# Where the score burst and the weighted sums stand in the rows of a dense attention stage, and where the sums are copied

## The chip, the cores and the metric

One core of a Trainium2 chip runs the whole program. A time is the device time of one execution in microseconds (us); lower is better. The engines that matter are PE (TensorE, matrix products), ACT (ScalarE), DVE (VectorE) and POOL (GpSimd). Each works through its own row of instructions in order, and they wait for each other through semaphores.

## What is computed

Two layers, each of attention and a feed-forward part, on 32 batches of 128 tokens with 256 values each. The change lies in the second layer's attention, which is dense (no mask), has 16 heads of 64, and reads the context in every batch:

```python
q = (query @ Wq + bq).reshape(b, sq, N_HEAD, KEY_DIM)
k = (key @ Wk + bk).reshape(b, key.shape[1], N_HEAD, KEY_DIM)
v = (value @ Wv + bv).reshape(b, value.shape[1], N_HEAD, VALUE_DIM)
scores = jnp.einsum('bqhd,bkhd->bhqk', q, k) / TEMP
attn = jax.nn.softmax(scores, axis=-1)
out = jnp.einsum('bhqk,bkhd->bqhd', attn, v).reshape(b, sq, N_HEAD * VALUE_DIM)
out = out @ Wo + bo + residual
mu = jnp.mean(out, axis=-1, keepdims=True)
var = jnp.var(out, axis=-1, keepdims=True)
return (out - mu) * jax.lax.rsqrt(var + EPS) * ln_gamma + ln_beta
```

Its input is a layer norm of the running sum x, and its result is added to x. Then comes a layer of routed experts.

## The kernel before

The program has four stages, one after the other: a masked attention, a feed-forward part, the dense attention (`attention1`, from about 650 us to 1293 us of the profiled execution) and the experts. Only `attention1` is touched.

`attention1` is a pipeline over the batches b = 0 to 31, with some steps ahead of it that only project, and some behind it that only finish. Each engine has a function `step(b, u, i)` whose calls are that engine's row, written out by hand; u is b modulo 4. `run_steps` writes the steps below 8 and from 28 on out one by one, and runs the twenty from 8 to 27 as a loop of four steps at a time, with b in a register.

The 16 heads of a batch are taken in four groups n of four heads. Scores are made in two bursts, g = 0 (groups 0 and 1) and g = 1 (groups 2 and 3), into the two banks of `ps_score`, and each group goes through this chain:

- PE, `scores(b, u, g)` (L1393): a burst of small products of `qT` and `kT`. It waits until the exponentials of both groups that used the two banks are done.
- DVE, `maxima(b, n)` (L1552, L1555): the row maximum, and from it `shift`.
- ACT, `exponentials(b, n)` (L1703): four ACTIVATEs that wait for `shift` and write `prob`, with the row sums.
- DVE, `divide(b, n)` (L1561, L1563): reciprocal and product.
- PE, `transposes(b, n)` (L1402), then ACT, `copy_probT(b, n)` (L1718).
- PE, `weighted(b, u, g)` (L1414): the weighted sums of two groups, into the one bank `ps_out`. It waits until `split_attn` has read the burst in front of it.
- ACT, `copy_attn(t, s, half)` (L1751) rounds `ps_out` into `attnT`, and DVE, `split_attn(t, s, half)` (L1588), takes what the rounding left over.
- PE, `output(b, u)` (L1493): 24 products with Wo for batch b - 1. It waits for both halves of that batch's `split_attn`.

In step b the groups 0 and 1 of batch b are carried up to `copy_probT`, while groups 2 and 3 of batch b - 1 are transposed and summed. In the same steps PE projects batch b + 2 (`queries` and `keys`, L1423, and `values`, L1453) through the two banks of `ps_proj`, emptied by ACT (`copy_projection`, L1725) and by DVE (`copy_values`, L1569, which waits for its `values`). `turn_x` (L1480), `copy_x` (ACT, L1733) and `split_x` (DVE, L1577) turn the input of batch b + 4; `turn_z`, `copy_z` (L1756) and `logits_of` (L1468) make the routing logits of batch b - 4. `add_residual` (L1606), `output_statistics` (L1610, L1613) and `normalise_output` (L1619 on) finish the output on DVE, with small helpers and the residual on POOL (L1357 to L1371). On odd steps `round_context` (ACT) and `split_context` (DVE, L1583) prepare context.

Of the kernel before, what the change touches and what calls it, by code (L numbers as in the profile page):

```python
# [1139 lines left out]
def attention1(nc, ident, mv2, rstd2, logits, wq_raw, wq_address, w, ctx_t, x2_dram, x3_dram, z_dram, finished):  # L1140
# [10 lines left out]
    with ExitStack() as stack:  # L1151
# [134 lines left out]
        with nc.Block() as block:  # L1286
# [97 lines left out]
            def _(pe):  # L1384
                def scores(b, u, g):
                    s, tok = u // 2, slice((u % 2) * P, (u % 2 + 1) * P)
                    if g == 0 and u % 2 == 0:
                        pe.wait_ge(qk_ready, BLKS * (b + 2))
                    if inside(b, 1, NB) or g == 1:
                        pe.wait_ge(exp_done, NU * b + 2 * g)  # L1390
                    for j, r in product(range(HB), range(2)):
                        blk, rows = HB * g + j, slice(r * KD, (r + 1) * KD)
                        last = pe.matmul(ps_score[:, r, j, :], qT[rows, s, blk, tok], kT[rows, s, blk, tok],  # L1393
                                         start=True, stop=True)
                    last.then_inc(scores_done, 1)
# [31 lines left out]
                def queries(b, u, j):  # L1427
                    if inside(b, *projects):
                        if isinstance(b, int) and b == projects[0]:
                            pe.wait_ge(w_split, 1)  # L1430
                        if j == 0 and u % 2 == 0:
                            pe.wait_ge(xnT_ready, b + 4)
                        if inside(b, -1, NB - 3):
                            pe.wait_ge(v_ready, 2 * b + 3 + j)
                        project(b, u, j, wq, xnT[:, 1 - u // 2])
# [35 lines left out]
                def turn_x(b, u):  # L1471
                    if inside(b, 4, NB - 5):
                        bank_after_logits(b)
                    elif inside(b, 2, 3):
                        pe.wait_ge(proj_ready, b - 1)
                    elif inside(b, FIRST + 1, 1):
                        pe.wait_ge(xnT_ready, b + 4)
                    pe.wait_ge(xn_ready, b + 5)
                    for k in range(ND):
                        last = pe.transpose(ps_aux[:, k * P:(k + 1) * P], xn[:, u % 2, k * P:(k + 1) * P], ident[:])  # L1480
                    last.then_inc(xnT_done, 1)
# [24 lines left out]
                def step(b, u, i):  # L1506
                    here, back = inside(b, 0, NB - 1), inside(b, 1, NB)
                    if here:
                        scores(b, u, 0)
                    queries(b, u, 0)  # L1510
                    if inside(b, 4, NB + 3):
                        turn_z(b, u)
                    if back:
                        transposes(b - 1, 2)
                        transposes(b - 1, 3)
                    queries(b, u, 1)
                    if inside(b, 4, NB + 3):
                        logits_of(b - 4)
                    keys(b, u, 0, i)
                    if inside(b, FIRST, NB - 5):  # L1520
                        turn_x(b, u)
                    if back:
                        weighted(b - 1, (u - 1) % 4, 1)
                    if here:
                        scores(b, u, 1)
                    keys(b, u, 1, i)
                    if here:
                        transposes(b, 0)
                        transposes(b, 1)
                    values(b, u, 0)  # L1530
                    if back:
                        output(b, u)
                    values(b, u, 1)
                    if here:
                        weighted(b, u, 0)

                run_steps(pe, step)

# [1 line left out]
            def _(dve):  # L1540
# [102 lines left out]
                def step(b, u, i):  # L1643

                    turn = [None if i is None else (i + 1 if u >= k else i) for k in range(4)]
                    turn_of_loop[0] = i
                    if isinstance(b, int) and b == projects[0]:
                        dve.wait_ge(bias_loaded, 16 * N_BIAS)
                    if inside(b, FIRST, NB - 5):
                        normalise(b + 4, u, None if i is None else i + 2)  # L1650
                    here, back = inside(b, 0, NB - 1), inside(b, 1, NB)
                    if back:
                        split_attn(b - 1, (u + 1) % 2, 0)
                    if here:
                        maxima(b, 0)
                        maxima(b, 1)
                    if inside(b, 2, NB + 1):
                        normalise_output(b - 2, (u + 2) % 4, turn[2])
                    if inside(b, 4, NB + 3):
                        route(b - 4)  # L1660
                    if here:
                        divide(b, 0)
                        divide(b, 1)
                    if isinstance(b, int) and (b, 0) in split_at:
                        rest_of_weights(split_at[b, 0])
                    if inside(b, FIRST, NB - 5):
                        split_x(b, u)
                    if inside(b, 3, NB + 2):
                        normalise_routed(b - 3, (u + 1) % 4, turn[3])
                    if back:  # L1670
                        split_attn(b - 1, (u + 1) % 2, 1)
                    if isinstance(b, int) and (b, 1) in split_at:
                        rest_of_weights(split_at[b, 1])
                    if u % 2 == 1 and inside(b, -3, NB - 5):
                        split_context(b, u)
                    if here:
                        maxima(b, 2)
                        maxima(b, 3)
                        divide(b, 2)
                    if inside(b, *projects):  # L1680
                        copy_values(b, u, 0)
                    if here:
                        divide(b, 3)
                    if back:
                        add_residual(b - 1, (u + 1) % 2)
                    if inside(b, *projects):
                        copy_values(b, u, 1)
                    if isinstance(b, int) and (b, 3) in split_at:
                        rest_of_weights(split_at[b, 3])
                    if back:  # L1690
                        output_statistics(b - 1, (u + 1) % 2)
# [4 lines left out]
            def _(act):  # L1696
# [61 lines left out]
                def step(b, u, i):  # L1758
                    if isinstance(b, int) and b == projects[0]:
                        act.wait_ge(bias_loaded, 16 * N_BIAS)  # L1760
                    here, back = inside(b, 0, NB - 1), inside(b, 1, NB)
                    if back:
                        copy_attn(b - 1, (u + 1) % 2, 0)
                    if here:
                        exponentials(b, 0)
                    if inside(b, 4, NB + 3):
                        copy_z(b - 4)
                    copy_projection(b, u, 0, qT, bq, 0)
                    if back:
                        copy_probT(b - 1, 2)  # L1770
                        copy_probT(b - 1, 3)
                    if here:
                        exponentials(b, 1)
                    copy_projection(b, u, 1, qT, bq, 0)
                    if isinstance(b, int) and split_at.get((b, 0)):
                        round_weights(split_at[b, 0])
                    copy_projection(b, u, 0, kT, bk, 2)
                    if inside(b, FIRST, NB - 5):
                        copy_x(b, u)
                    if back:  # L1780
                        copy_attn(b - 1, (u + 1) % 2, 1)
                    if isinstance(b, int) and split_at.get((b, 1)):
                        round_weights(split_at[b, 1])
                    if u % 2 == 1 and inside(b, -3, NB - 5):
                        round_context(b, u, i)
                    if here:
                        exponentials(b, 2)
                    copy_projection(b, u, 1, kT, bk, 2)
                    if here:
                        copy_probT(b, 0)  # L1790
                        copy_probT(b, 1)
                        exponentials(b, 3)
                    if isinstance(b, int) and split_at.get((b, 3)):
                        round_weights(split_at[b, 3])
# [599 lines left out]
```

## Time and profile before

| | us |
|---|---|
| median of 3 runs | 1632.46 (1629.01 to 1633.26) |
| the profiled execution | 1626.76 |
| its span, first to last instruction | 1625.0 |
| PE busy in the span | 1341.5 (83%) |
| DVE busy | 1220.5 (75%) |
| ACT busy | 1032.5 (64%) |
| POOL busy | 488.9 (30%) |

Shares of busy time are means over four unlike stages. For one stage the table of busy times by stretch and the timeline of each engine are read: what stands behind what, how far apart two starts are, and which instruction an idle engine was waiting for. PEld in such a table is PE's loading of weights. PE's ends are modelled, so for PE the distance between starts says more than its busy time.

### The profile page before, as it was taken

Reading aid. Unit: us, or ns where it says so; the run is one execution under the profiler, and the core shown is the slowest. Engines: PE = TensorE matmul, PEld = TensorE weight load, DVE = VectorE, ACT = ScalarE, POOL = GpSimd, SP = SyncE. Lnnn points to the kernel's source line nnn. Section 1 sums busy time; section 2 is a strip of 40 time slices with the busy share of each in tenths; the row PEclk is TensorE's granted clock in tenths of the full one; section 3 lists DMA queues with packets and bytes.
Section 4 is the critical chain, followed back from the end, with each engine's and each line's share of the span. In section 5 each row is a group of like instructions: output and inputs, shape, how many; then the busy total and the mean of one; then the engine's idle time right before and its main releaser. Section 6 shows DMA issues by size and latency. Waiting matters only on the chain. (4 is left out here: it accounts for less than half of the span.)

```text
span 1625.0 us, 36516 instructions
## 1 busy us (share of the span) xinstructions
PE 1341.5 (83%) x11579; PEld 1174.6 (72%) x11579; DVE 1220.5 (75%) x2159; ACT 1032.5 (64%) x2751; POOL 488.9 (30%) x734
## 2 busy tenths in 40 slices
PE   3688888599961059699999999999999649998897
PEld 2465555488841059689999998989898549988897
DVE  5777777668778988467777777777777679877776
ACT  2588788555588445377766666666676328877675
POOL 2433433100000001302222222222222256667665
PEclk9799999799996579799999999999999769999999
DMA  6411111000051013501111111111110257111110
GB/s 199 146 37 34 35 35 34 12 0 0 0 168 69 8 45 115 192 1 44 34 34 34 34 44 32 32 32 32 32 39 24 81 213 267 49 40 43 43 47 20
DMA packets 66243, 96.78 MB, mean 60 GB/s; under 512 B 10213, under 2 KB 57326, under 8 KB 63345
## 3 DMA queue, kind: packets, MB, share of 16 engines
q1 hardware_dynamic: 60546, 83.16, 15.4%
q0 software_dynamic: 5616, 12.60, 2.4%
q8 instruction: 44, 0.72, 0.2%
q14 instruction: 37, 0.30, 0.1%
HBM read 76.57 MB, written 21.90 MB: 61 GB/s over the span
## 5 line engine op out<-in xcount | busy, mean ns | idle before, releaser
L1703 ACT ACTIVATE c_w_raw<-c_ps_score,c_shift 128x128 f32<-128x128 f32 x512 | 184.7, 399 | 132.2 <-DVE c_shift L1555 129.6
L2096 PE MATMUL d_ps_hT<-d_zT,d_w_tile 128*128 128x128 f32 x1248 | 148.2, 278 | 1.9 <-DVE d_zT L2201 1.9
L2096 PEld LDWEIGHTS d_ps_hT<-d_zT,d_w_tile 128*128 128x128 f32 x1248 | 145.2, 195 | 2.6 <-DVE d_zT L2201 2.6
L840 PE MATMUL b_ps<-b_down_high,b_inner 128*128 128x256 f32 x384 | 71.7, 290 | 88.3 <-DVE b_inner L1122 88.3
L2267 ACT ACTIVATE d_h<-d_ps_hT,d_b1T 128x128 f32<-128x128 f32 x312 | 88.8, 367 | 64.8 <-PE d_ps_hT L2096 62.6
L2109 PE MATMUL d_ps_y<-d_w_parts,d_hT 128*128 128x256 f32 x936 | 126.3, 293 | 1.8 <-DVE d_res L2228 1.8
L840 PEld LDWEIGHTS b_ps<-b_down_high,b_inner 128*128 128x128 f32 x384 | 61.3, 196 | 88.7 <-issue 88.7
L1369 POOL TENSOR_TENSOR c_var_o<-c_mv_o,c_eps 128x1 f32<-128x1 f32 x32 | 6.8, 213 | 394.0 <-DVE c_mv_o L1613 394.0
L484 DVE TENSOR_REDUCE a_row_max<-a_ps_score 128x8 f32<-128x1024 f32 x64 | 78.0, 1219 | 57.9 <-PE a_ps_score L395 57.9
L1703 ACT ACTIVATION_READ_ACCUMULATOR c_w_raw<-c_ps_score,c_shift 128x1 f32 x512 | 121.4, 237 | 0.0
L2109 PEld LDWEIGHTS d_ps_y<-d_w_parts,d_hT 128*128 128x128 f32 x936 | 119.0, 198 | 2.4 <-DVE d_res L2228 2.0
L2220 DVE TENSOR_TENSOR d_w_parts<-d_w,d_w_parts 128x1024 fp32r<-128x1024 f32 x78 | 95.7, 1228 | 28.2 <-ACT d_w_parts L2279 26.5
L1423 PE MATMUL c_ps_proj<-c_ctxT,c_wk 128*128 128x256 f32 x768 | 106.8, 289 | 4.2 <-ACT c_qT L1725 2.9
L577 ACT ACTIVATE a_probT<-a_ps_probT 128x512 f32<-128x512 f32 x128 | 71.5, 626 | 57.1 <-PE a_ps_probT L406 56.9
L1423 PE MATMUL c_ps_proj<-c_xnT,c_wq 128*128 128x256 f32 x768 | 105.9, 289 | 1.0 <-DVE c_xnT L1577 1.0
L2279 ACT ACTIVATE d_w_parts<-d_w 128x1024 fp32r x78 | 82.2, 1054 | 34.2 <-PE d_ps_y L2109 28.8
L1423 PEld LDWEIGHTS c_ps_proj<-c_ctxT,c_wk 128*128 128x128 f32 x768 | 94.5, 191 | 10.5 <-issue 3.3
L1453 PE MATMUL c_ps_proj<-c_wv,c_ctxT 128*128 128x512 f32 x384 | 100.7, 399 | 1.1 <-DVE c_wv L1595 1.1
L1423 PEld LDWEIGHTS c_ps_proj<-c_xnT,c_wq 128*128 128x128 f32 x768 | 94.6, 192 | 5.1 <-issue 1.4
L1561 DVE RECIPROCAL c_inv_sum<-c_row_sum 128x4 f32<-128x4 f32 x128 | 22.5, 176 | 99.5 <-ACT c_w_raw L1703 99.1
L866 ACT ACTIVATE b_act<-b_ps 128x512 f32 (+1 forms) x96 | 56.7, 601 | 61.9 <-PE b_ps L805 57.2
L1493 PEld LDWEIGHTS c_ps_aux<-c_wo,c_attnT 128*128 128x128 f32 x768 | 92.1, 188 | 4.4 <-issue 1.9
(263 smaller groups left out, 3747.4 us busy)
## 6 DMA issues: line engine op xcount, KB each, us to landing
d_w<-w_in SPq DMA_DIRECT2D x16, 1024.0 KB, 12.2
b_x_space<-w_in SPq DMA_DIRECT2D x16, 512.0 KB, 3.5
a_x<-x_in SPq DMA_DIRECT2D x4, 1024.0 KB, 8.0
a_keys<-ctx_blocks_in SPq DMA_DIRECT2D x128, 32.0 KB, 2.1
a_v_raw<-ctx_in SPq DMA_DIRECT2D x4, 1024.0 KB, 9.0
x_scratch<-a_x SPq DMA_DIRECT2D x32, 128.0 KB, 1.7
b_x_space<-x_scratch SPq DMA_DIRECT2D x32, 128.0 KB, 2.3
x_scratch<-b_x_space SPq DMA_DIRECT2D x32, 128.0 KB, 1.9
```

Of the source, the lines that this page charges most:

```text
L484: dve.tensor_reduce(row_max[:, half, :], ps_score[:, half], AX_X, ALU.max).then_inc(max_done, 1)
L577: act.activation(probT[:, q], ps_probT[:, q % 2], ACT.Copy).then_inc(probT_ready, 1)
L840: last = pe.matmul(ps[:, t, 0:D], inner[:, s, a, f, t * P:(t + 1) * P], down_parts[b][:, f, :], start=(j == 0), stop=(j == NF * len(PARTS) ...
L1423: last = pe.matmul(ps_proj[:, j, h * PT:(h + 1) * PT], weights[:, a, k, blk * P:(blk + 1) * P], src[:, c, k, :], start=(n == 0), stop=(n = ...
L1453: last = pe.matmul(ps_proj[:, j, :], ctxT[:, 1 - u // 2, a, k, tok], wv[:, c, k, j * BANK:(j + 1) * BANK], start=(n == 0), stop=(n == ND * ...
L1493: last = pe.matmul(ps_aux[:, 0:D], attnT[:, s, a, blk, :], wo[:, c, blk, :], start=(n == 0), stop=(n == BLKS * len(PARTS) - 1))
L1703: last = act.activation(prob[:, n, j, :], ps_score[:, n % 2, j, :], ACT.Exp, scale=float(KD) ** -0.5, bias=shift[:, n, j:j + 1], accum_out ...
L2096: last = pe.matmul(ps_hT[:, f, :], w1_tile[:, half, k, n * P:(n + 1) * P], zT[:, s, k, :], start=(k == 0), stop=(k == ND - 1))
L2109: last = pe.matmul(ps_y[:, 0:D], hT[:, s, a, f, :], w2_parts[:, half, b, n, :], start=(f == 0 and (a, b) == PARTS[0]), stop=(f == FB - 1 a ...
L2220: dve.tensor_tensor(w2_parts[:, half, 1], w2[:, e, half * FB // 2:(half + 1) * FB // 2, :], w2_parts[:, half, 0].bitcast(F32), ALU.subtrac ...
L2267: act.activation(h[:, f, :], ps_hT[:, f, :], ACT.Relu, bias=b1T[:, e, f:f + 1]).then_inc(h_ready, 1)
L2279: act.activation(w2_parts[:, half, 0], w2[:, e, half * FB // 2:(half + 1) * FB // 2, :], ACT.Copy)\
```

## The change

It moves calls inside the `step` functions of PE, DVE and ACT. No instruction is added or taken away, and no size, buffer or semaphore count changes.

- PE: `scores(b, u, 1)` now stands ahead of `weighted(b - 1, ..., 1)`. `weighted(b, u, 0)`, which was the last call of step b, is now in step b + 1 behind its `scores(b + 1, u, 0)`.
- DVE: `split_attn` of half 0 moves from ahead of `maxima(b, 0)` to behind `maxima(b, 1)`; that of half 1 moves from ahead of `split_context` and `maxima(b, 2)` to behind `maxima(b, 3)`, ahead of `divide(b, 2)`.
- ACT: `copy_attn` of half 0 moves behind `exponentials(b, 0)`; that of half 1 moves from ahead of `round_context` to behind `exponentials(b, 2)`.

```diff
@@ PE @@
                     if here:
                         scores(b, u, 0)
+                    if back:
+                        weighted(b - 1, (u - 1) % 4, 0)
                     queries(b, u, 0)
...
+                    if here:
+                        scores(b, u, 1)
                     if back:
                         weighted(b - 1, (u - 1) % 4, 1)
-                    if here:
-                        scores(b, u, 1)
                     keys(b, u, 1, i)
...
                     values(b, u, 1)
-                    if here:
-                        weighted(b, u, 0)
@@ DVE @@
-                    if back:
-                        split_attn(b - 1, (u + 1) % 2, 0)
                     if here:
                         maxima(b, 0)
                         maxima(b, 1)
+                    if back:
+                        split_attn(b - 1, (u + 1) % 2, 0)
...
-                    if back:
-                        split_attn(b - 1, (u + 1) % 2, 1)
...
                     if here:
                         maxima(b, 2)
                         maxima(b, 3)
+                    if back:
+                        split_attn(b - 1, (u + 1) % 2, 1)
+                    if here:
                         divide(b, 2)
@@ ACT @@
+                    if here:
+                        exponentials(b, 0)
                     if back:
                         copy_attn(b - 1, (u + 1) % 2, 0)
-                    if here:
-                        exponentials(b, 0)
...
-                    if back:
-                        copy_attn(b - 1, (u + 1) % 2, 1)
...
                     if here:
                         exponentials(b, 2)
+                    if back:
+                        copy_attn(b - 1, (u + 1) % 2, 1)
```

In the rows below REGISTER_ALU and ISA are the register and wait work of the loop. ACT in the first step of the loop, from `copy_x` (c_xnT) on; before:

```order
L1733 ACTIVATE c_xnT<-c_ps_aux 128x2x128
L1748 REGISTER_ALU
L1751 ACTIVATE c_attnT<-c_ps_out 128x512
L1699 REGISTER_ALU
L1701 REGISTER_ALU
L1703 ACTIVATE c_w_raw,c_row_sum<-c_ps_score,c_shift 128x128 x4
L1722 REGISTER_ALU
L1725 ACTIVATE c_kT<-c_ps_proj,c_bk 128x256 x2
```

ACT at the same place, after the change (line numbers of ACT are one higher there):

```order
L1734 ACTIVATE c_xnT<-c_ps_aux 128x2x128
L1700 REGISTER_ALU
L1702 REGISTER_ALU
L1704 ACTIVATE c_w_raw,c_row_sum<-c_ps_score,c_shift 128x128 x4
L1749 REGISTER_ALU
L1752 ACTIVATE c_attnT<-c_ps_out 128x512
L1723 REGISTER_ALU
L1726 ACTIVATE c_kT<-c_ps_proj,c_bk 128x256 x2
```

The copy of the sums (c_attnT) stood directly behind `copy_x`; now the four ACTIVATEs of `exponentials(b, 2)` are between them. DVE in the same step, from z on; before:

```order
L1640 TENSOR_SCALAR c_z<-c_x,c_mv,c_rstd 128x256
L1586 REGISTER_ALU
L1588 TENSOR_TENSOR c_attnT<-c_ps_out,c_attnT 128x512
L1551 REGISTER_ALU
L1552 TENSOR_REDUCE c_row_max<-c_ps_score 128x4
L1553 REGISTER_ALU
L1555 TENSOR_SCALAR c_shift<-c_row_max 128x4
L1552 TENSOR_REDUCE c_row_max<-c_ps_score 128x4
L1553 REGISTER_ALU
L1555 TENSOR_SCALAR c_shift<-c_row_max 128x4
L1561 RECIPROCAL c_inv_sum<-c_row_sum 128x4
```

DVE at the same place, after:

```order
L1640 TENSOR_SCALAR c_z<-c_x,c_mv,c_rstd 128x256
L1551 REGISTER_ALU
L1552 TENSOR_REDUCE c_row_max<-c_ps_score 128x4
L1553 REGISTER_ALU
L1555 TENSOR_SCALAR c_shift<-c_row_max 128x4
L1552 TENSOR_REDUCE c_row_max<-c_ps_score 128x4
L1553 REGISTER_ALU
L1555 TENSOR_SCALAR c_shift<-c_row_max 128x4
L1586 REGISTER_ALU
L1588 TENSOR_TENSOR c_attnT<-c_ps_out,c_attnT 128x512
L1561 RECIPROCAL c_inv_sum<-c_row_sum 128x4
```

`split_attn` of half 1 (c_attnT) went from ahead of the two maxima to behind them. PE across the border of the first and the second step of the loop, before:

```order
L1453 MATMUL c_ps_proj<-c_wv,c_ctxT 128x512 x6
L1410 ISA
L1414 MATMUL c_ps_out<-c_w_raw,c_v 64x128 x8
L1390 REGISTER_ALU
L1393 MATMUL c_ps_score<-c_kT,c_qT 128x128 x8
L1434 REGISTER_ALU
L1423 MATMUL c_ps_proj<-c_xnT,c_wq 128x256 x12
```

PE at the same place, after:

```order
L1453 MATMUL c_ps_proj<-c_wv,c_ctxT 128x512 x6
L1390 ISA
L1393 MATMUL c_ps_score<-c_kT,c_qT 128x128 x8
L1410 REGISTER_ALU
L1414 MATMUL c_ps_out<-c_w_raw,c_v 64x128 x8
L1434 REGISTER_ALU
L1423 MATMUL c_ps_proj<-c_xnT,c_wq 128x256 x12
```

Between the last values and the first queries the score burst (c_ps_score) and the weighted sums (c_ps_out) have changed places; the projections around them stand as they did.

## Rows read from the trace of the kernel before

**Rows 1.** Busy us by stretch: PE, PEld, DVE, ACT, POOL; clock, DMA share, GB/s.

```profile
900.00:1000.00 100.00, 98.85 (x908) 89.91 (x907) 73.63 (x173) 67.19 (x261) 21.92 (x40) 1.00 0.12 34
```

**Rows 2.** Timeline of PE: start, us taken, instruction; steps 1, 7, 9, 10 and 27.

```profile
720.50 2.88 PE L1493 MATMUL c_ps_aux<-c_wo,c_attnT 128*128 128x256 f32 x24
...
828.96 2.88 PE L1493 MATMUL c_ps_aux<-c_wo,c_attnT 128*128 128x256 f32 x24
...
865.80 2.88 PE L1493 MATMUL c_ps_aux<-c_wo,c_attnT 128*128 128x256 f32 x24
868.52 1.54 PE L1453 MATMUL c_ps_proj<-c_wv,c_ctxT 128*128 128x512 f32 x6
869.98 1.09 PE L1414 MATMUL c_ps_out<-c_w_raw,c_v 128*64 128x128 f32 x16
871.01 1.16 PE L1393 MATMUL c_ps_score<-c_kT,c_qT 64*128 64x128 f32 x16
...
876.44 0.61 PE L1468 MATMUL c_ps_aux<-c_wr,c_zT 128*128 128x8 f32 x4 [0.24 <-ACT c_zT L1756]
...
884.82 2.88 PE L1493 MATMUL c_ps_aux<-c_wo,c_attnT 128*128 128x256 f32 x24
...
1203.40 2.99 PE L1493 MATMUL c_ps_aux<-c_wo,c_attnT 128*128 128x256 f32 x24
```

**Rows 3.** Timeline of ACT in step 10: exponentials 0 and 1, copies, exponentials 2 and 3.

```profile
874.60 0.37 ACT L1703 ACTIVATE c_w_raw<-c_ps_score,c_shift 128x128 f32<-128x128 f32 x1 [2.88 <-DVE c_shift L1555]
...
875.99 0.39 ACT L1756 ACTIVATE c_zT<-c_ps_aux 128x256 f32<-128x256 f32 x1
...
877.92 0.42 ACT L1703 ACTIVATE c_w_raw<-c_ps_score,c_shift 128x128 f32<-128x128 f32 x1
...
880.73 0.50 ACT L1733 ACTIVATE c_xnT<-c_ps_aux 128x256 fp32r<-128x256 f32 x1
880.99 0.72 ACT L1751 ACTIVATE c_attnT<-c_ps_out 128x512 fp32r<-128x512 f32 x1
883.52 0.37 ACT L1703 ACTIVATE c_w_raw<-c_ps_score,c_shift 128x128 f32<-128x128 f32 x1 [1.81 <-DVE c_shift L1555]
...
886.57 0.42 ACT L1703 ACTIVATE c_w_raw<-c_ps_score,c_shift 128x128 f32<-128x128 f32 x1
```

**Rows 4.** Timeline of DVE from step 9's last copy of values to step 10's.

```profile
870.90 0.68 DVE L1569 TENSOR_TENSOR c_v<-c_ps_proj,c_bv 128x512 f32<-128x512 f32 x1
...
872.02 0.18 DVE L1613 BATCH_NORM_AGGREGATE c_mv_o<-c_stats_o 128x2 f32<-128x6 f32 x1
...
872.61 0.68 DVE L1588 TENSOR_TENSOR c_attnT<-c_ps_out,c_attnT 128x512 fp32r<-128x512 f32 x1
873.21 0.68 DVE L1552 TENSOR_REDUCE c_row_max<-c_ps_score 128x4 f32<-128x512 f32 x1
873.92 0.57 DVE L1555 TENSOR_SCALAR c_shift<-c_row_max 128x4 f32<-128x4 f32 x1
...
882.52 0.68 DVE L1552 TENSOR_REDUCE c_row_max<-c_ps_score 128x4 f32<-128x512 f32 x1
...
889.32 0.68 DVE L1569 TENSOR_TENSOR c_v<-c_ps_proj,c_bv 128x512 f32<-128x512 f32 x1
```

**Rows 5.** Timeline of ACT: the first ACTIVATE of exponentials 2 in steps 11 to 13.

```profile
902.54 0.37 ACT L1703 ACTIVATE c_w_raw<-c_ps_score,c_shift 128x128 f32<-128x128 f32 x1 [1.89 <-DVE c_shift L1555]
...
921.11 0.37 ACT L1703 ACTIVATE c_w_raw<-c_ps_score,c_shift 128x128 f32<-128x128 f32 x1 [1.81 <-DVE c_shift L1555]
...
940.14 0.37 ACT L1703 ACTIVATE c_w_raw<-c_ps_score,c_shift 128x128 f32<-128x128 f32 x1 [1.89 <-DVE c_shift L1555]
```

**Rows 6.** Timeline of DVE: its first instruction in step 12, a new turn of the loop.

```profile
910.26 0.42 DVE L1546 TENSOR_SCALAR c_xn<-c_x_early,mv,rstd 128x256 f32<-128x256 f32 x1 [0.62 <-issue]
```

**Rows 7.** Timeline of POOL in step 10: two operations of the residual.

```profile
873.07 0.61 POOL L1357 TENSOR_TENSOR c_xn_bo<-c_x_late,mv 128x256 f32<-128x256 f32 x1
873.85 0.61 POOL L1361 TENSOR_TENSOR c_xn_bo<-c_xn_bo,rstd 128x256 f32<-128x256 f32 x1 [0.17 <-POOL c_xn_bo L1357]
```

## The prediction, made before the changed kernel ran

> **What bounds the stage now.** The table of busy times by stretch comes first: in 100 us of the dense attention PE is busy 98.85 us at the full clock, DVE 73.63 and ACT 67.19 [rows 1]. Taken alone this says that PE is the bound. The timelines say more. In step 10 `output` starts 19.02 us after that of step 9 (884.82 - 865.80), and PE waited visibly only once, for `copy_z`, before `logits_of` [rows 2]. From step 1 to step 7 six steps took 108.46 us, 18.08 each [rows 2], so PE alone can do a step in less. From step 7 to step 27 twenty steps took 374.44, 18.72 each [rows 2]. Something other than PE sets the pace once the early slack is used up.
>
> To find it, follow one instruction round to itself, here the second `copy_values` of a step (I call it V), through the waits of ACT and DVE. V at 870.90; statistics, aggregate at 872.02; `split_attn` 872.61; `maxima` 873.21; shift 873.92 [rows 4]; first exponential 874.60 (X), 3.70 us behind V. ACT then has no idle time until `copy_x` at 880.73 [rows 3]. DVE waits for its end (881.23), splits x, makes z, splits the sums and is at `maxima(b, 2)` at 882.52 [rows 4]; the exponentials 2 (E) start at 883.52 [rows 3], 8.92 behind X. E to exponentials 3 is 3.05 [rows 3], and the next V is at 889.32 [rows 4], 5.80 behind E. 3.70 + 8.92 + 5.80 = 18.42. PE is not in this circle. An odd step has `split_context` in it as well: E to E is 19.02, then 18.57 and 19.03 [rows 3, 5]; so the odd extra is 0.59 or 0.60. Four steps are 75.0 us, and twenty 375: the circle of ACT and DVE explains the 374.44. **The bound is a circle of waits between ACT and DVE, with PE some 0.3 us a step behind it**: from step 7 to step 9, before the early slack was gone, the loop took 36.84 us, 18.42 a step [rows 2], which I take as PE's own pace there.
>
> **What the change does to that circle.** Two DVE instructions leave it: `split_attn` half 0 from between the aggregate and `maxima(b, 0)`, and half 1 from between z and `maxima(b, 2)`, 0.60 each (873.21 - 872.61) [rows 4]. Two ACT instructions come in: `copy_attn` half 0 between exponentials 0 and 1, half 1 between exponentials 2 and 3. ACT's copy costs 0.48 of the row, an estimate: 0.60 for the copy from an idle start would be the upper bound, and 0.26 (what `copy_x` took of the row, 880.99 - 880.73, with half the columns) the lower [rows 3]; I take 0.48, near twice the lower. On this account: 18.42 - 1.20 + 0.96 = 18.18. Besides, the shift of 873.92 took 0.57 and ended (874.49) with a POOL operation that had started at 873.85 [rows 4, 7]. Without `split_attn` it would start 1.30 behind the aggregate instead of 1.90, at a time when the POOL operation of 1.05 to 1.66 behind the aggregate runs [rows 7], so it still waits, but about 0.2 less. That makes about 18.0, less than PE's 18.4. If that were all, the stage would gain.
>
> The Trainium skill (SBUF — State Buffer, "SBUF: two separate sides") says that DVE and GpSimd share a port pair which one of them holds for a whole instruction. It agrees with the shift's end, and by it the shift could lose all 0.4 us only if POOL's operations moved too.
>
> **What the change does to `output`.** `output(b)` waits for `split_attn` half 1, and this now waits for a copy behind exponentials 2. From E: four exponentials 1.39 (875.99 - 874.60), copy 0.72, a gap of 0.03, split 0.68 [rows 3, 4]: ready at E + 2.82. With 0.05 for the semaphore and 0.05 for a PE that starts from rest (between 0 and 0.15, no row shows it alone) `output` cannot start before E + 2.92. Before, it started at E + 1.30 (884.82 - 883.52) [rows 2, 3]. Work on PE between cannot hide it: PE runs in order, and `output` stands in front of the `values` whose copy is V.
>
> So PE enters the circle. With O for the start of `output`: the last `values` start at O + 2.72 and end at O + 4.26 (868.52 + 1.54 - 865.80) [rows 2]; V at O + 4.31; X 2.90 later (3.70 less 0.60 less 0.2), at O + 7.21; E 8.80 later (8.92 less 0.60 plus 0.48), at O + 16.01; next O at E + 2.92 = **18.93**. The divide chain would ask for V at E + 5.80 + 0.48 = E + 6.28 and finds it at E + 7.23, so `output` sets it. An odd step adds 0.59: 19.52. Mean 19.23. The first step of each turn has an idle 0.62 on DVE [rows 6], which the circle keeps: 0.54 more than the usual gap, 0.13 a step. In the loop 19.36.
>
> What else is moved past what: `scores(b, 0)` now starts at O + 4.18 and is ready before `maxima(b, 0)` at O + 6.0; its own wait, for exponentials 3, ends at E + 5.1, before. `weighted(b - 1, 0)` is done near O + 6.4 and its copy is asked for at O + 8.6. No DMA or SP wait moves; PE does the same products, and its granted clock was 1.00 [rows 1], with 95% of the time still busy. DVE stands still behind `maxima(b, 1)` until the copy of half 0 is done, X + 2.1, and has normalise_output, route and two divides queued behind it: about 4.1 us of work, done at X + 6.9; the next thing, `split_x`, could not start before X + 7.1. So this costs nothing, with 0.2 to spare.
>
> **The sum.** Loop: 20 x 19.36 = 387.2 against 374.44: +12.8. Steps 2 to 7: PE and the circle are a little shorter there (no z in the first), I take 19.0 against 18.08, 6 steps: +5.5 (3 to 7.5). The first wait of all: E comes 0.92 earlier than before, so `output` is late by 2.92 - 0.92 - 1.30 = 0.7. Steps 28 and 29 have no `copy_x` and PE sets them: nothing, and nothing is caught up. Behind them the projections are gone and a score burst that is 1.03 earlier (871.01 - 869.98) [rows 2] may save up to 1.03 a step for two steps: -1. Sum +18.0: 1626.8 + 18.0 = 1644.8 for an execution like the profiled one. This one lies 5.7 below the median of the runs, so against the median: **1650.5 us**. About 0.3% (4.9 us) is what a measurement can tell from no change.
>
> **Rivals.**
> - *The copies are hidden (faster).* If `output` did not have to wait, say because exponentials 2 start so much earlier that E + 2.92 is before PE's own turn, PE's 18.42 would be the bound: 20 x 0.3 = -6, and -1 at the end, 1625.5. It needs E at 2.9 before `output`; E is 1.30 before it now and gains 0.92. The rows speak against it.
> - *PE is the bound (no change).* 98.85 of 100 us busy, the same products. 1632. The Trainium skill (Perfetto Trace Analysis, "Identifying the Most-Contended Engine") says to take the engine with the highest occupancy first, for PE by its weight loads; those are 89.91 of 100 here, the highest too [rows 1], and by that rule the time stays at 1632. The step of 19.02 against 18.08 speaks against it.
> - *DVE falls behind as well (slower still).* If its standstill behind `maxima(b, 1)` lasts 0.4 longer than I think, or a POOL operation stretches one of the things behind it by 0.4 as it did the shift, `split_x` starts 0.2 to 0.4 late in each of some 26 steps: +5 to +10, 1658.
> - *`scores(b, 1)` waits for exponentials 1.* Its cover, `weighted`, now stands behind it. Exponentials 1 end at X + 3.32 + 0.48 + 1.39 + 0.2 = X + 5.4; from there PE has 5.9 us up to `output`, X + 11.3, and the circle has it at X + 11.7. Hidden by 0.4, so a wait that shows but sets nothing.
>
> **Chances.** The forecast 0.62; slower still 0.14; a smaller loss (the early steps have slack, the waits cost less), 1638 to 1643, 0.07; no change 0.07; hidden and faster 0.10. Faster by over 0.3%: 0.10. Within 0.3%: 0.08, with the edge of the small loss. Slower: 0.82. The range leaves out the faster case and the far end of the slowest: 1635 to 1661.
>
> **What would show it.** Right: a wait of PE before L1493 for `split_attn` (DVE, L1588) in nearly every step, 0.5 to 1.1 us; distance of outputs near 19.4; no wait left before the logits; V on DVE with idle time ahead of it that PE ended; the idle time of ACT before exponentials 2 down from 1.8 to about 1.7 only. Wrong: no such wait, outputs 18.4 apart; then the copies found room that I did not see. If PE's waits sit before L1393 in their place, the fourth rival was the bound.

## The result, and the profile after

The changed kernel takes 1652.63 us (median of 4 runs, 1643.56 to 1654.32) against 1632.86 for the kernel before beside it (1629.01 to 1634.94). The ratio is 1.0119, with a 95% interval of 1.0096 to 1.0142: slower, by 19 to 20 us. Five more rounds (the last experiment) gave 1.011 (1.0089 to 1.013). The forecast was 1650.5, slower, 1635 to 1661. All medians are of fast runs: one execution of the kernel with copy 1 early took 3254 us and one of PE alone 3394, and neither is counted.

Its profiled execution took 1651.97 us, with a span of 1650.2. The table of busy times by stretch has the same columns as [rows 1]:

```profile
900.00:1000.00 100.00, 97.20 (x889) 86.88 (x887) 69.29 (x167) 65.14 (x253) 23.49 (x42) 1.00 0.10 32
```

PE at the same full clock is busy 1.65 us less in 100. That looks harmless, and it stands for a stage that is 3.5% longer: ends of PE are modelled, so a wait of 1.2 us of its weight loads shows as 0.7 in its products. The table of waits (engine and what waited, line, for whom; us in total, times, longest) for the loop, steps 8 to 27, first of before and then of the changed kernel:

```profile
PE c_ps_aux L1468 <- ACT c_zT L1756: 2.2, 7, 0.4
```

```profile
PE c_ps_aux L1493 <- DVE c_attnT L1588: 7.1, 10, 0.7
PE c_ps_aux L1480 <- DVE logits L1601: 1.9, 5, 0.5
```

The same table for the weight loads of the changed kernel has the wait in nearly every step, as the prediction asked:

```profile
PEld c_ps_aux L1493 <- DVE c_attnT L1588: 15.4, 19, 1.2
...
PEld c_ps_score L1393 <- ACT c_w_raw L1704: 4.3, 20, 0.3
```

The wait for `copy_z` before the logits is gone, and `output` (L1493) waits for `split_attn` (L1588) in its place. DVE's own waits in the loop of the changed kernel:

```profile
DVE c_attnT L1588 <- ACT c_attnT L1752: 51.6, 40, 1.3
DVE c_inv_sum L1561 <- ACT c_w_raw L1704: 19.9, 20, 1.0
DVE c_v L1569 <- PE c_ps_proj L1453: 18.2, 20, 1.0
```

The third row is the circle of the prediction closed through PE: the second `copy_values` of every step (V) now waits 0.9 us for the last `values`, and it waited for no engine before. The PE timeline of step 10 against [rows 2]:

```profile
872.58 3.10 PE L1493 MATMUL c_ps_aux<-c_wo,c_attnT 128*128 128x256 f32 x24 [0.73 <-DVE c_attnT L1588]
...
875.51 1.54 PE L1453 MATMUL c_ps_proj<-c_wv,c_ctxT 128*128 128x512 f32 x6
...
876.97 1.16 PE L1393 MATMUL c_ps_score<-c_kT,c_qT 64*128 64x128 f32 x16
...
885.43 1.16 PE L1393 MATMUL c_ps_score<-c_kT,c_qT 64*128 64x128 f32 x16
...
891.57 3.10 PE L1493 MATMUL c_ps_aux<-c_wo,c_attnT 128*128 128x256 f32 x24
```

And ACT, DVE and POOL in the same step, against [rows 3], [rows 4] and [rows 7]:

```profile
877.08 0.69 DVE L1569 TENSOR_TENSOR c_v<-c_ps_proj,c_bv 128x512 f32<-128x512 f32 x1 [0.92 <-PE c_ps_proj L1453]
...
879.26 0.61 POOL L1357 TENSOR_TENSOR c_xn_bo<-c_x_late,mv 128x256 f32<-128x256 f32 x1
...
879.52 0.38 DVE L1555 TENSOR_SCALAR c_shift<-c_row_max 128x4 f32<-128x4 f32 x1
...
880.01 0.37 ACT L1704 ACTIVATE c_w_raw<-c_ps_score,c_shift 128x128 f32<-128x128 f32 x1 [5.12 <-DVE c_shift L1555]
...
888.80 0.37 ACT L1704 ACTIVATE c_w_raw<-c_ps_score,c_shift 128x128 f32<-128x128 f32 x1 [1.69 <-DVE c_shift L1555]
...
890.18 0.61 ACT L1752 ACTIVATE c_attnT<-c_ps_out 128x512 fp32r<-128x512 f32 x1
...
890.83 0.69 DVE L1588 TENSOR_TENSOR c_attnT<-c_ps_out,c_attnT 128x512 fp32r<-128x512 f32 x1 [1.34 <-ACT c_attnT L1752]
```

One turn of the circle reads: `output` (O) 872.58, V 877.08, first exponential (X) 880.01, exponentials 2 (E) 888.80, copy 890.18, split 890.83, next `output` 891.57. It is 18.99 long, where 18.93 was forecast.

The starts of `output` in steps 1, 7 and 27, against [rows 2], give the length of each piece:

```profile
722.11 2.96 PE L1493 MATMUL c_ps_aux<-c_wo,c_attnT 128*128 128x256 f32 x24 [0.56 <-issue]
...
834.09 3.07 PE L1493 MATMUL c_ps_aux<-c_wo,c_attnT 128*128 128x256 f32 x24 [0.54 <-DVE c_attnT L1588]
...
1221.03 3.09 PE L1493 MATMUL c_ps_aux<-c_wo,c_attnT 128*128 128x256 f32 x24 [0.73 <-DVE c_attnT L1588]
```

| piece of the stage | before, us | after, us | difference |
|---|---|---|---|
| first scores to `output` of step 1 | 26.69 | 27.81 | +1.1 |
| steps 2 to 7 | 108.46 | 111.98 | +3.5 |
| the loop, steps 8 to 27 | 374.44 | 386.94 | +12.5 |
| steps 28 to 32 | 76.24 | 78.67 | +2.4 |
| last `output` to the experts' first product | 15.75 | 17.04 | +1.3 |
| all of them | 601.58 | 622.43 | +20.9 |

The spans differ by 25.2. Of the other 4.3, 3.9 lie in the experts, whose code is the same: from their first product to the end it is 329.6 us in the trace of before and 333.5 in that of after, and 325.9 to 333.6 in the ten traces of the experiments, seven of them between 331.2 and 332.6. So before was some 2 us short there and after some 2 long, by scatter between executions. That accounts for about 2 of the 5.7 us by which the profiled execution of before lay below the median; the rest was not looked for.

### The profile page after: what moved, and what is told of

Its sections match the earlier page's. It is cut to its first block and busy times, and to the rows that moved or that the text cites. A ratio compares the mean times of both kernels' runs of the same rounds, so it can differ in the third digit from the quotient of the medians.

```text
span 1650.2 us, 36516 instructions
## 1 busy us (share of the span) xinstructions
PE 1353.5 (82%) x11579; PEld 1176.7 (71%) x11579; DVE 1204.7 (73%) x2159; ACT 1027.3 (62%) x2751; POOL 491.1 (30%) x734
## 5 line engine op out<-in xcount | busy, mean ns | idle before, releaser
L1493 PEld LDWEIGHTS c_ps_aux<-c_wo,c_attnT 128*128 128x128 f32 x768 | 94.7, 193 | 27.2 <-DVE c_attnT L1588 16.5
L1493 PE MATMUL c_ps_aux<-c_wo,c_attnT 128*128 128x256 f32 x768 | 100.6, 287 | 15.2 <-DVE c_attnT L1588 14.1
L1588 DVE TENSOR_TENSOR c_attnT<-c_ps_out,c_attnT 128x512 fp32r<-128x512 f32 x64 | 44.2, 691 | 77.6 <-ACT c_attnT L1752 77.6
```

The costliest lines, as they stand in the source:

```text
L1493: last = pe.matmul(ps_aux[:, 0:D], attnT[:, s, a, blk, :], wo[:, c, blk, :], start=(n == 0), stop=(n == BLKS * len(PARTS) - 1))
```

## Experiments

Theory: `output` waits for a copy that stands behind exponentials 2, and through the last `values` this wait closes a circle of about 19.2 us a step. Rivals: the score burst of half 1 has lost its cover on PE; DVE's standstill behind `maxima(b, 1)`; and that the copies cost nothing. "Loop" below is always from `output` of step 7 to that of step 27 in the kernel's own trace, 374.44 us in before. All edits are against the kernel before unless it is said otherwise, and every kernel computes the whole result.

**Half 0 alone.**

```diff
@@ PE: weighted(b, u, 0) from the end of the step to behind the next scores(b, u, 0) @@
@@ DVE @@
-                    if back:
-                        split_attn(b - 1, (u + 1) % 2, 0)
                     if here:
                         maxima(b, 0)
                         maxima(b, 1)
+                    if back:
+                        split_attn(b - 1, (u + 1) % 2, 0)
@@ ACT: copy_attn half 0 behind exponentials(b, 0) @@
```

> Only half 0 of the change: weighted(b, u, 0) behind the next scores, split_attn half 0 behind maxima 1, copy_attn half 0 behind exponentials 0. Half 1 as before. If output's wait for the late copy of half 1 is what costs (my theory), nothing of it is here: the circle of ACT and DVE is 18.42 - 0.60 - 0.2 + 0.48 = 18.1, PE's 18.42 is the bound, distance of outputs 18.4, time about 6 us below before, near 1627. If DVE's standstill behind maxima 1 costs, the distance is over 19 and the time 1640 or more. If the PE order of the second burst costs, as before, 1633.

Measured: 1628.94 (ratio 0.9978, 0.9965 to 0.9991), loop 373.57. This half is not the loss. But it brings only 0.9 us of the 6 in the loop, so something new holds PE. The waits of PE in the loop name it, and one of its cases in the timeline (step 12, a new turn of the loop) shows what it is queued behind:

```profile
PE c_ps_aux L1480 <- DVE logits L1601: 3.5, 9, 0.5
```

```profile
914.98 0.69 DVE L1588 TENSOR_TENSOR c_attnT<-c_ps_out,c_attnT 128x512 fp32r<-128x512 f32 x1 [0.83 <-ACT c_attnT L1751]
...
917.82 0.17 DVE L1601 TENSOR_TENSOR logits<-c_ps_aux,c_br 128x8 f32 x1
...
918.12 0.43 PE L1480 MATMUL c_ps_aux<-ident,c_xn 128*128 128x128 f32 x2 [0.47 <-DVE logits L1601]
```

`turn_x` on PE may not write `ps_aux` before DVE's `route` has read the logits. `route` is behind `normalise_output`, that behind `split_attn`, and that waits 0.83 us for ACT's copy. The standstill of DVE does cost, through the bank of the logits. The table of waits shows up to 0.5 us in 9 of 20 steps, 3.5 in sum, and that is not all of it: in all 20 steps `turn_x` starts 0.29 or 0.30 behind `route`, whether a wait is shown or not (with one split moved, below, it starts up to 0.90 behind it). The V of steps 8, 9 and 10 show what sets the pace by turns:

```profile
853.79 0.69 DVE L1569 TENSOR_TENSOR c_v<-c_ps_proj,c_bv 128x512 f32<-128x512 f32 x1 [0.46 <-PE c_ps_proj L1453]
...
872.49 0.68 DVE L1569 TENSOR_TENSOR c_v<-c_ps_proj,c_bv 128x512 f32<-128x512 f32 x1
...
890.99 0.69 DVE L1569 TENSOR_TENSOR c_v<-c_ps_proj,c_bv 128x512 f32<-128x512 f32 x1 [0.32 <-PE c_ps_proj L1453]
```

To 872.49 it is the circle of ACT and DVE, with nothing of PE waited for: 18.70, which is the 18.10 of the expectation plus the 0.60 of `split_context` that I had left out when I set 18.1 against PE. To 890.99 it is 18.50, where that circle would ask for only 18.10: here V waits for PE, and PE had been held by `route`. Two steps are 37.2, against 36.5 at PE's own pace of 18.24 (read below from the kernel with one split moved).

**Half 1 alone.**

```diff
@@ PE @@
-                    if back:
-                        weighted(b - 1, (u - 1) % 4, 1)
                     if here:
                         scores(b, u, 1)
+                    if back:
+                        weighted(b - 1, (u - 1) % 4, 1)
@@ DVE: split_attn half 1 behind maxima(b, 3) @@
@@ ACT: copy_attn half 1 behind exponentials(b, 2) @@
```

> Only half 1 of the change: scores(b, u, 1) ahead of weighted, split_attn half 1 behind maxima 3, copy_attn half 1 behind exponentials 2. Half 0 as before. My theory: the circle goes through output and still holds split_attn half 0, V at O + 4.50, X 3.70 later, E 8.32 later, next O 2.77 later: 19.29 in even steps, 19.88 in odd, mean 19.6, loop 392 us against 374, time near 1657, slower than the whole change. If scores(b, u, 1) waiting for exponentials 1 is the cause: like the whole change, 1652. If DVE's standstill of half 0 is: as before, 1633.

Measured: 1660.32 (1.0168, 1.0144 to 1.0192), loop 392.52 where 392 was worked out. Half 1 alone is worse than both halves, as a circle that still holds `split_attn` half 0 must be. The waits between 840 and 1230 us, nearly all of the loop:

```profile
PE c_ps_score L1393 <- ACT c_w_raw L1704: 9.2, 20, 0.5
PE c_ps_aux L1493 <- DVE c_attnT L1588: 6.6, 9, 0.7
```

The burst of scores that lost its cover waits 0.5 us in all 20 steps. By the circle it sets nothing: the steps are 19.31 and 19.89 long where 19.29 and 19.88 were worked out without it. What PE loses there, it would lose again before L1493.

**ACT and DVE changed, PE as before.**

```diff
@@ DVE and ACT as in the change; PE untouched @@
```

> ACT and DVE in the changed order, PE in the order of before. My theory: output still waits for the copy behind exponentials 2, so the time is that of the whole change, near 1652, with the wait before L1493 and outputs 19.4 apart. If the order of the bursts on PE (scores(b, u, 1) without its cover) is the cause: as before, 1633.

Measured: 1664.24 (1.02, 1.0185 to 1.0214), loop 390.20. With PE in its old order the wait before `output` is there all the same, so the order of the bursts is not the cause. It is even 12 us worse than the whole change by the medians, 3.3 of them in the loop, 3.4 in steps 2 to 7 (115.33) and 4.7 in steps 28 to 32 (83.32), which I had not expected. For the loop DVE's waits show why:

```profile
DVE c_row_max L1552 <- PE c_ps_score L1393: 4.9, 15, 0.3
```

Freed of `split_attn`, `maxima(b, 0)` comes early enough to wait for a score burst that stands behind the weighted sums. I had put it at O + 6.0 and not asked when the burst would end in PE's old order: O + 2.93 + 1.47 + 1.03 + 1.16 = O + 6.6. So the PE part of the change pays, once the rest of it is there. What it saves outside the loop was not followed.

**DVE alone changed.**

```diff
@@ DVE @@
-                    if back:
-                        split_attn(b - 1, (u + 1) % 2, 0)
                     if here:
                         maxima(b, 0)
                         maxima(b, 1)
+                    if back:
+                        split_attn(b - 1, (u + 1) % 2, 0)
...
-                    if back:
-                        split_attn(b - 1, (u + 1) % 2, 1)
...
                     if here:
                         maxima(b, 2)
                         maxima(b, 3)
+                    if back:
+                        split_attn(b - 1, (u + 1) % 2, 1)
+                    if here:
                         divide(b, 2)
```

> Only DVE in the changed order: both split_attn behind the maxima; ACT and PE as before. My theory: the circle loses 0.60 twice and some 0.2 of the shift's wait, 17.0 in even steps, so PE's 18.42 is the bound; the late split of half 1 asks for output at E + 1.5 at the earliest, and E comes 1.4 earlier. Outputs 18.4 apart, loop 368 us against 374, time near 1627, below before by 0.35%. If PE were the bound before already, 1633. If a late split_attn by itself holds output up: slower, 1640.

Measured: 1621.20 (0.9946, 0.9925 to 0.9967), loop 366.01. Faster than before. The circle of ACT and DVE was the bound, and the late split of half 1 by itself holds next to nothing up: the loop is 1.2 us longer than with split 0 alone (last but one experiment).

**The whole change, with one copy moved back ahead of its exponentials.** Against the changed kernel:

```diff
@@ ACT @@
+                    if back:
+                        copy_attn(b - 1, (u + 1) % 2, 1)
                     if here:
                         exponentials(b, 2)
-                    if back:
-                        copy_attn(b - 1, (u + 1) % 2, 1)
```

> The whole change, but ACT's copy_attn half 1 is ahead of exponentials 2 (behind round_context) in place of behind them. PE and DVE as in the change. My theory: the copy is asked for at X + 7.7, when its weighted sums are done, and ends before exponentials 2 start at X + 8.8; split_attn stands behind maxima 3 and output can start at E + 1.5. The wait before L1493 goes, and the loop falls from 387 us to 366 to 374, time near 1628: one moved row is the whole loss. If the PE order of the second burst or DVE's standstill behind maxima 1 costs: like the whole change, 1650.

Measured: 1629.90 (0.9976, 0.9954 to 0.9997), loop 371.95. One call on ACT carries 15 us of the loop. This is the cleanest evidence for the theory: nothing else differs. The steps are 18.5 long and not PE's 18.24, and their rows (`output`, V, X, `scores(b, 1)`, `output`) say why:

```profile
869.21 2.88 PE L1493 MATMUL c_ps_aux<-c_wo,c_attnT 128*128 128x256 f32 x24
...
873.50 0.69 DVE L1569 TENSOR_TENSOR c_v<-c_ps_proj,c_bv 128x512 f32<-128x512 f32 x1 [0.29 <-PE c_ps_proj L1453]
...
876.43 0.37 ACT L1704 ACTIVATE c_w_raw<-c_ps_score,c_shift 128x128 f32<-128x128 f32 x1 [4.49 <-DVE c_shift L1555]
...
881.86 1.16 PE L1393 MATMUL c_ps_score<-c_kT,c_qT 64*128 64x128 f32 x16
...
887.73 2.88 PE L1493 MATMUL c_ps_aux<-c_wo,c_attnT 128*128 128x256 f32 x24
```

O to V 4.29, V to X 2.93, X to the scores 5.43 (they wait for exponentials 1), scores to O 5.87: 18.52. The wait itself is hidden in the rows of PE's products, and the table of its weight loads has it in every step of the loop:

```profile
PEld c_ps_score L1393 <- ACT c_w_raw L1704: 4.3, 20, 0.3
```

The fourth rival of the prediction is a second circle, and it surfaces as soon as the first is gone. In the changed kernel the same wait is there, of the same size, and sets nothing.

**PE alone changed.**

```diff
@@ PE as in the change; ACT and DVE untouched @@
```

> PE alone in the changed order, ACT and DVE as before. My theory: copy_attn half 1 stands ahead of exponentials 2 and split_attn ahead of maxima 2, and both wait for weighted sums that come one burst later: about +0.5 us a step on the circle, and up to 0.25 by half 0, 19.0 to 19.2 in even steps, loop 385 to 390 us, time 1645 to 1650. If only output's wait for the late copy costs, and the PE order costs nothing by itself: as before, 1632.

Measured: 1670.63 (1.0238, 1.0211 to 1.0265), loop 392.44: the slowest of all, some 20 us above what was expected, of which the loop had 2 to 7. (The profiled execution is one of 1662.99; its experts took 325.9 us, less than in any other trace.) Between 840 and 1230 us:

```profile
PE c_ps_score L1393 <- ACT c_w_raw L1703: 9.7, 20, 0.5
PE c_ps_aux L1468 <- ACT c_zT L1756: 4.7, 15, 0.4
```

```profile
904.51 0.60 ACT L1751 ACTIVATE c_attnT<-c_ps_out 128x512 fp32r<-128x512 f32 x1 [3.20 <-PE c_ps_out L1414]
905.14 0.69 DVE L1588 TENSOR_TENSOR c_attnT<-c_ps_out,c_attnT 128x512 fp32r<-128x512 f32 x1 [0.84 <-ACT c_attnT L1751]
...
914.18 0.60 ACT L1751 ACTIVATE c_attnT<-c_ps_out 128x512 fp32r<-128x512 f32 x1 [0.56 <-PE c_ps_out L1414]
```

PE's own waits set nothing here: V waits for no engine in the whole loop. It is the circle of ACT and DVE that grew, because both copies still stand ahead of their exponentials, and both splits ahead of their maxima, while the sums come one burst later. Half 0 makes V to X 4.52 in this step in place of 3.70, and that in every second step; half 1 makes X to E 9.99 in place of 9.52, and some 0.5 in every step. 10 x 0.8 and 20 x 0.47 are 17.4 of the 18.0 us that the loop lost. The expectation had half 0 at 0.25 at most. Steps 2 to 7 (116.22 against 108.46) and 28 to 32 (86.53 against 76.24) lost 18 us more; I had priced neither, and the traces of them were not followed.

**The whole change, with copy_attn half 0 left ahead of exponentials 0.** Against the changed kernel:

```diff
@@ ACT @@
+                    if back:
+                        copy_attn(b - 1, (u + 1) % 2, 0)
                     if here:
                         exponentials(b, 0)
-                    if back:
-                        copy_attn(b - 1, (u + 1) % 2, 0)
```

> The whole change, but ACT's copy_attn half 0 stays ahead of exponentials 0. My theory: ACT is idle there for 5 us and the sums are done 0.9 us before X, so the copy costs nothing there and 0.48 on the circle where the change has it. The circle still goes through output: 19.0 - 0.48 = 18.5 in even steps, 19.1 in odd, loop near 377 us, time near 1642. If the copy is not on the circle: like the whole change, 387 and 1652.

Measured: 1637.51 (1.0034, 1.0019 to 1.0048), loop 377.72 where 377 was worked out. This weighs the disputed cost by itself: a copy of 0.48 us of ACT's row, once a step on the circle, is 9.2 us in 20 steps.

**Both copies ahead of their exponentials, the rest as in the change.**

```diff
@@ the two ACT edits above together, against the changed kernel @@
```

> PE and DVE as in the change, ACT with copy_attn half 0 ahead of exponentials 0 (as before) and half 1 just ahead of exponentials 2, behind round_context. My theory: neither copy is on the circle, PE's own pace of 18.24 to 18.4 is the bound, loop 366 to 368 us, time near 1621, like DVE alone in the changed order. If scores(b, u, 1) without its cover costs by its wait for exponentials 1: loop above 370.

Measured: 1621.88 (0.9933, 0.9916 to 0.995), loop 365.19. With both copies off the circle, PE and DVE in the changed order gain. By the same working the second circle is down by 0.48 too, to 18.0 (an estimate), and 16 of the 20 steps take PE's 18.24.

**One call moved from before.**

```diff
@@ DVE @@
-                    if back:
-                        split_attn(b - 1, (u + 1) % 2, 0)
                     if here:
                         maxima(b, 0)
                         maxima(b, 1)
+                    if back:
+                        split_attn(b - 1, (u + 1) % 2, 0)
```

> One call moved from before: DVE's split_attn half 0 behind maxima 1. Everything else as before. My theory: the circle of ACT and DVE loses 0.60 and some 0.2 of the shift's wait, 17.6 in even steps and 18.2 in odd, both under PE's own 18.24 to 18.4, so the loop is 366 to 368 us and the time near 1622, like all of DVE in the changed order. If each of the two splits had its own share of the gain: half of it, loop 370, 1627.

Measured: 1621.13 (0.9935, 0.992 to 0.995). Its rows of `output` in steps 7 and 27, and its busy times:

```profile
829.76 2.88 PE L1493 MATMUL c_ps_aux<-c_wo,c_attnT 128*128 128x256 f32 x24
...
1194.56 2.88 PE L1493 MATMUL c_ps_aux<-c_wo,c_attnT 128*128 128x256 f32 x24
```

```profile
900.00:1000.00 100.00, 100.00 (x940) 91.42 (x940) 74.31 (x177) 67.72 (x263) 22.32 (x42) 1.00 0.12 34
```

364.80 us for 20 steps, 18.24 each, and no wait of PE in the loop. Here PE is the bound, and this is the whole gain: the kernels that also move the second split, or that and the PE order, are no faster. It is the version to keep, since it has the least in it; its time is level with that of DVE alone and of both copies early.

**The changed kernel once more.**

> The changed kernel once more, in five rounds beside before, for a narrower ratio: the stage is 21 us longer in its trace, which is a ratio of 1.013; the first four runs gave 1.0119 with 0.0023 either side.

Measured: 1649.61 (1.011, 1.0089 to 1.013), loop 387.06.

| kernel | median, us | loop, us |
|---|---|---|
| before | 1630.7 to 1632.9 | 374.44 |
| the change | 1652.63 | 386.94 |
| half 0 alone | 1628.94 | 373.57 |
| half 1 alone | 1660.32 | 392.52 |
| ACT and DVE | 1664.24 | 390.20 |
| PE alone | 1670.63 | 392.44 |
| change, copy 1 early | 1629.90 | 371.95 |
| change, copy 0 early | 1637.51 | 377.72 |
| change, both early | 1621.88 | 365.19 |
| DVE alone | 1621.20 | 366.01 |
| split 0 alone | 1621.13 | 364.80 |

## Why the prediction was right, and where it was off

The direction, the mechanism and the size held. That the sum came within some 2 us of the median is in part luck: outside the loop it was 2.0 too high in steps 2 to 7 and 4.7 too low at the end, and inside it several terms were off against each other.

- *The bound before is a circle of ACT and DVE.* Shown: taking one split, 0.6 us of DVE, out of it sped the loop up by 9.6 us with PE untouched.
- *PE's own pace of 18.42.* Wrong: it is 18.24. The two steps I read it from were already at the circle's 18.42: X to X is 18.42 (855.58 - 837.16). In both, the keys behind the logits start 2.56 behind X, as they do in step 10, where the timeline of the weight loads shows them waiting for ACT:

```profile
837.16 0.37 ACT L1703 ACTIVATE c_w_raw<-c_ps_score,c_shift 128x128 f32<-128x128 f32 x1 [2.19 <-DVE c_shift L1555]
839.72 1.65 PE L1423 MATMUL c_ps_proj<-c_ctxT,c_wk 128*128 128x256 f32 x12
...
855.58 0.37 ACT L1703 ACTIVATE c_w_raw<-c_ps_score,c_shift 128x128 f32<-128x128 f32 x1 [2.28 <-DVE c_shift L1555]
858.14 1.65 PE L1423 MATMUL c_ps_proj<-c_ctxT,c_wk 128*128 128x256 f32 x12
...
877.16 1.45 PEld L1423 LDWEIGHTS c_ps_proj<-c_ctxT,c_wk 128*128 128x128 f32 x12 [0.21 <-ACT c_qT L1725]
```

  So the faster rival was too small: PE-bound means 9.6 us less in the loop, not 6. The 18.08 of steps 2 to 7 was the row to doubt it by; it mixes four steps of 18.24 to 18.26 with two shorter ones.
- *E to `output` 2.92.* 2.77. The copy behind exponentials took 0.61 and not the 0.72 it had behind `copy_x`, which is most of the 0.15.
- *`output` to the last `values` 2.72.* 2.93 (875.51 - 872.58): a burst of `output` that starts after a wait takes 3.10, against 2.88. The restart was priced at 0.05. The two errors cancel but for 0.06.
- *V to X 2.90 and X to E 8.80.* 2.93 and 8.79. The shift took 0.38 in place of 0.57, the 0.2 less that the prediction took, and ended at 879.90 with POOL's operation (879.26 + 0.61 = 879.87), as in the trace of before it ended at 874.49 with the one that ended at 874.46.
- *The loop 387.2.* 386.94. The first step of a turn took 0.2 to 0.35 more than another even step, where 0.54 had been put; the other steps took up to 0.1 more than forecast. Steps 2 to 7: +3.5 for a forecast of +5.5. The first wait: +1.1 for 0.7.
- *The end: -1.* Wrong in sign, +3.7. The score bursts did come earlier, and waited for exponentials; and in these steps too `output` waits for its late split. The three rows of PE in steps 30 and 31:

```profile
1268.44 1.82 PE L1393 MATMUL c_ps_score<-c_kT,c_qT 64*128 64x128 f32 x16 [1.76 <-ACT c_w_raw L1704]
...
1274.15 3.06 PE L1493 MATMUL c_ps_aux<-c_wo,c_attnT 128*128 128x256 f32 x24 [0.95 <-DVE c_attnT L1588]
...
1289.68 4.41 PE L1493 MATMUL c_ps_aux<-c_wo,c_attnT 128*128 128x256 f32 x24 [2.50 <-DVE c_attnT L1588]
```

  The circle had not been followed where the projections end, and there nothing covers it.
- *DVE's standstill costs nothing.* Nearly: its 0.2 to spare was counted to `split_x`, but the first to need something queued behind it is `turn_x`, which waits for `route`. Five waits of 0.4 us on average in the changed kernel, hidden by the larger circle; in half 0 alone it is what V waits for in every second step, and a part of the gain that was missing.
- *`scores(b, 1)` waits for exponentials 1, hidden by 0.4.* Right, and shown by the kernel with copy 1 early. It is hidden by 0.3: there X to the next `output` takes 5.43 + 5.87 = 11.30 this way, and 11.56 (891.57 - 880.01) in the changed kernel.
- *PE is the bound (no change).* Wrong for before, at 98.85 of 100; right for the kernel with one split moved, at 100.00. The Trainium skill (Perfetto Trace Analysis, "Identifying the Most-Contended Engine") says to optimise the engine with the highest occupancy first, and for PE to go by the weight loads. Taken alone this points at PE here, 89.91 of 100 by its weight loads, and the traces do not agree: both the loss and the 10 us gain came from what stands on a chain of waits, with PE's products the same.

Not tried: what the change costs in the steps before the loop piece by piece; the +1.1 and +3.5 are only read from the trace.

## What to carry to other kernels

Where three engines hand work round, write down the chain from one instruction back to itself a step later, sum it from the trace, and compare it with the pace of the busiest engine: at 98.85% busy that engine was not the bound. An order of calls is then priced by what it puts on that chain and what it takes off, and a result that another engine waits for must not stand behind a burst that it doesn't need. Of six moves here one alone gave all of the gain, and two copies moved back took away all of the loss, so a bundle of moves is worth taking apart. The parts do not simply add up: PE's two moves cost 18.0 us of the loop alone and save 3.3 when DVE and ACT are changed with them.

## What the runs showed of the hardware

A burst of 24 products that begins after PE had stood waiting ran 0.2 us longer than one that begins in the stream: 3.10 against 2.88, and what follows it starts 2.93 instead of 2.72 behind its start, at a granted clock of 1.00 both times. Expected was 0.05. The kernel with copy 0 early shows the same 3.09 to 3.10; why the burst is longer was not tried.
